# A message-passing layer's prologue: order of TensorE's and ScalarE's work, two weight loads and one group of gathers moved

## The chip, the cores and the metric

One NeuronCore of a Trainium2 chip runs the whole kernel. The metric is the device time of one execution in microseconds; a kernel's time is the median of several executions. Engines: TensorE (PE, with its weight loads as PEld), VectorE (DVE), ScalarE (ACT), GpSimd (POOL) and SyncE (SP), which here only issues DMAs. Transfers run on 16 DMA engines that all queues share.

## What is computed

1250 nodes with 512 features, 40000 edges sorted by destination, 64 features per edge. Cut to what matters:

```python
h = relu(layernorm(x))                                  # 1250 x 512
edge = concat([h[src], h[dst], edge_attr])              # 40000 x 1088
messages = mish(mish(edge @ W1 + b1) @ W2 + b2)         # 40000 x 512
agg = segment_sum(messages, dst)
u = mish(concat([h, agg]) @ W3 + b3)
x1 = x + layernorm(h + u @ W4 + b4) * gamma + beta
h2 = relu(layernorm(x1))
out = x1 + relu(segment_sum(((h2 @ U * s) @ Vt)[src] * w, dst) + bias)
```

## The kernel before

**Stages.** A prologue (time 0 to about 76 us) normalises x and makes two tables in DRAM: A = h @ W1[0:512], gathered later by `src`, and B = h @ W1[512:1024] + b1, read later by `dst`. The edge stage (about 76 to 1390 us) walks the edges in groups of 512 (four subtiles of 128): it gathers rows of A by an indirect DMA on GpSimd, transposes them on TensorE, adds B's rows and the edge part in the same PSUM bank (`bp`), applies mish, multiplies by W2 (`bm`, 12 products a subtile), applies mish again and sums by destination. Node and convolution stages end the kernel. Products are kept exact by splitting each operand in a high and a low part (`...h`, `...l`): a table row block is three times four products.

**Order.** Each engine has its own program, written out by hand, and executes in order; semaphores join them. x is cut in 10 chunks of 128 nodes, chunk numbers c = 0 to 9, that arrive in three batches, `BATCH` = chunks 0-1, 2-4 and 5-9.

**The prologue's program per chunk.** ScalarE makes relu(c) in place (`xs`/`hs`, L661). TensorE transposes it (L704, 4 instructions, bank `pT[c % 2]`). ScalarE copies the bank to `nTh` (`evac`, L470), VectorE subtracts for `nTl` (L614). TensorE makes the A product of the chunk (`table_a`, L681, 12 matmuls to `pA[c % 2]`: 4 with nTh and w1h, 4 with nTl, 4 with w1l). ScalarE copies `pA` to `ta` (`store_a`, L480) and SyncE issues its store to DRAM (L737). In TensorE's program the transposes of chunk c stand in front of the A product of chunk c-1. Ten B products (`pB`) follow the ten A products, and VectorE splits and stores them (L461 to L465, stores L761 and L762).

**VectorE between chunks.** After `nTl` of chunk c, VectorE runs the steps that the dictionary `between` lists for c: the statistics of the next batch (`variances`, `scales`), `windows` (waits for `dsti` and `dcoli`), `iotas`, the split of W1's second half (`w1_hi`, `w1_lo`), of W2 (`w2_hi`, `w2_lo`), `columns` (waits for `scoli` and `wcol`) and `bases`.

**SyncE's queue.** x batch 0, W1's first half (1 MB), x batches 1 and 2, x's tail of 98 rows, `dsti` (79 rows of 2 KB), `dcoli`, and then the A stores in order of chunk, with other loads behind some of them: W1's second half behind store 0, `wcraw` and W2 (1 MB) behind store 1, a wait for the windows and their store behind store 3, `scoli`, `wcol` and `b1b` behind store 4, `base_b` behind store 5. GpSimd issues zero fills of the result tables, one per transposed chunk (`agg_tab` for chunks 0 to 4, `M_tab` for 5 to 8).

**GpSimd in the edge stage.** In slot s it makes the low part of the hidden value of subtile s+4 (`low`, L985), then gathers for a group two ahead: for the third group (subtiles 8 to 11) rows 0 and 1 in slot -1, row 2 in slot 0, row 3 in slot 1, each behind the slot's `low`. The gathers of a group land on one semaphore, and TensorE starts on the group when all four have landed.

Of the kernel before, what the change touches and what calls it, by code (L numbers as in the profile page):

```python
# [23 lines left out]
ACT = mybir.ActivationFunctionType  # L24
# [4 lines left out]
KC = H // P  # L29
N = 1250  # L30
NCH = -(-N // P)
# [3 lines left out]
SUB = 4  # L35
# [181 lines left out]
def gnn_two_layers(nc, x, src_idx, dst_rows, src_cols, dst_cols, eaT, ew_cols, W1, b1, W2, b2, W3, b3, W4, b4,  # L217
# [39 lines left out]
    with ctx:  # L257
# [128 lines left out]
        with st:  # L386
# [52 lines left out]
            c_ta = sem("c_ta")  # L439
            c_tb = sem("c_tb")  # L440
            c_pad = sem("c_pad")
            v = {}
            prologue = Work()

# [22 lines left out]
            def evac(e, c):  # L467
                i = c % 2
                e.wait_ge(c_tr, c + 1)
                e.activation(nTh[:, :, c * P:(c + 1) * P], pT[i][:, :].rearrange("p (k n) -> p k n", k=KC),  # L470
                             ACT.Copy).then_inc(c_hi, 1)
                if c >= 1:
                    store_a(e, c - 1)

            def store_a(e, c):
                i = c % TA
                e.wait_ge(c_A, c + 1)
                if c >= TA:
                    e.wait_ge(q_sa[i], 16 * (c // TA))
                e.activation(ta[i][:], pA[c % 2][:, :], ACT.Copy).then_inc(c_ta, 1)  # L480

            @prologue.on("vector")
            def _(e):
                def link(ins):
                    c_v.inc(ins)
# [6 lines left out]
                def variances(i):  # L492

                    c0, c1 = BATCH[i]
                    e.wait_ge(q_x[i], (16, 16, 32)[i])
                    for c in range(c0, c1):
                        c_v.inc(e.bn_stats(stats[:, c, :], xs[:, c, :]))
                    later()
                    for c in range(c0, c1):
                        c_v.inc(e.bn_aggr(mv[:, c, :], stats[:, c, :]))  # L500
                    later()
                    link(e.tensor_scalar(var[:, c0:c1], mv[:, c0:c1, 1], LN_EPS, None, ALU.add))
                    v["var", i] = c_v.n
# [7 lines left out]
                                                ALU.mult, ALU.mult))  # L511
                    v["rstd", i] = c_v.n

                def w1_hi(i):

                    k = slice(i * KC, (i + 1) * KC)
                    e.wait_ge(q_w1[i], 16)
                    link(e.tensor_copy(w1h[:, k, :], w1raw[:, k, :]))
                    v["w1h", i] = c_v.n

                def w1_lo(i):

                    k = slice(i * KC, (i + 1) * KC)
                    c_v.inc(e.tensor_tensor(w1l[:, k, :], w1raw[:, k, :], w1h[:, k, :], ALU.subtract))
                    v["w1l", i] = c_v.n

# [25 lines left out]
                def w2_hi():  # L552

                    e.wait_ge(q_w2, 3 * 16)
                    c_v.inc(e.tensor_scalar(W2h[:], W2raw[:], -1.0, None, ALU.mult))
                    c_v.inc(e.tensor_copy(eaW2[:], wcraw[:]))
                    for i in range(2):
                        c_v.inc(e.tensor_copy(eaW1[i][64:128, :], wcraw[64:128, :]))

                def w2_lo():  # L560

                    later()
                    c_v.inc(e.scalar_tensor_tensor(W2l[:], W2raw[:], -1.0, W2h[:], ALU.mult, ALU.subtract))
                    c_v.inc(e.tensor_tensor(eaW2[64:128, :], wcraw[64:128, :], eaW2[64:128, :], ALU.subtract))

# [25 lines left out]
                def columns():  # L591
# [7 lines left out]
                    c_v.inc(e.scalar_tensor_tensor(scol8[:], rem[:], -float(EC), scolf[:], ALU.mult, ALU.add))  # L599
                    c_v.inc(e.tensor_tensor(wcol_hl[:, :, 1], wcol[:], wcol_hl[:, :, 0], ALU.subtract))  # L600

                between = {0: [lambda: variances(1), lambda: scales(1)], 1: [lambda: variances(2)], 2: [windows],
                           3: [lambda: scales(2), iotas], 4: [lambda: w1_hi(1)], 5: [lambda: w1_lo(1)], 6: [w2_hi],
                           7: [w2_lo], 8: [columns], 9: [bases]}

                e.memset(xs[:, NCH - 1, :], 0.0).then_inc(c_pad, 1)
                variances(0)
                scales(0)
                w1_hi(0)
                w1_lo(0)  # L610
                for c in range(NCH):
                    i = c % 2
# [34 lines left out]
            @prologue.on("scalar")  # L647
            def _(e):
                e.preload_act_table_set("natural_log_exp_and_others")
                for c in range(NCH):  # L650
                    for i in range(len(BATCH)):
                        c0, c1 = BATCH[i]
                        if c == (0, 2, 4)[i]:

                            e.wait_ge(c_v.sem, v["var", i])
                            e.activation(lnv[:, c0:c1], var[:, c0:c1], ACT.Ln).then_inc(c_a, 1)
                            e.wait_ge(c_a, 2 * i + 1)
                            e.activation(rstd[:, c0:c1], lnv[:, c0:c1], ACT.Exp, scale=-0.5).then_inc(c_a, 1)
                        if c == c0:
# [3 lines left out]
                    if c >= 1:  # L663
                        evac(e, c - 1)
                evac(e, NCH - 1)
                store_a(e, NCH - 1)

            @prologue.on("tensor")
            def _(e):
                e.wait_ge(c_g.sem, 4)  # L670

                def table(c, half, bank):

                    n = 0
                    for a, w, part in ((nTh, w1h, "w1h"), (nTl, w1h, None), (nTh, w1l, "w1l")):
                        if part and c == 0:
                            e.wait_ge(c_v.sem, v[part, half])
                        if half == 0 and a is nTl:
                            e.wait_ge(c_lo, c + 1)
                        for k in range(KC):  # L680
                            last = e.matmul(bank[:, :], a[:, k, c * P:(c + 1) * P], w[:, half * KC + k, :],  # L681
                                            start=n == 0, stop=n == 3 * KC - 1)
                            n += 1
                    return last

                def table_a(c):

                    e.wait_ge(c_hi, c + 1)
                    if c >= 2:
                        e.wait_ge(c_ta, c - 1)  # L690
                    table(c, 0, pA[c % 2]).then_inc(c_A, 1)

                def table_b(c):

                    if c >= TB:
                        e.wait_ge(c_tb, 3 * (c - TB) + 1)
                    table(c, 1, pB[c % TB]).then_inc(c_B, 1)

                for c in range(NCH):
                    e.wait_ge(c_hT, c + 1)  # L700
                    if c >= 2:
# [4 lines left out]
                    if c >= 1:  # L706
                        table_a(c - 1)
                table_a(NCH - 1)
                for c in range(NCH):
                    table_b(c)  # L710

            @prologue.on("sync")
            def _(e):
# [15 lines left out]
                        w1_half(0)  # L729
                e.wait_ge(c_pad, 1)  # L730
                e.dma_start(xs[0:NTAIL, NCH - 1, :], x[(NCH - 1) * P:N, :]).then_inc(q_x[-1], 16)
                e.dma_start(dsti[:], dst_rows).then_inc(q_dst, 16)
                e.dma_start(dcoli[:], dst_cols).then_inc(q_dst, 16)

                for c in range(NCH):
                    e.wait_ge(c_ta, c + 1)
                    e.dma_start(A_d[c * P:(c + 1) * P, :], ta[c % TA][:]).then_inc(q_sa[c % TA], 16)  # L737
                    if c == 0:
                        w1_half(1)
                    if c == 1:  # L740
                        for a, b in HALF:
                            e.dma_start(wcraw[a:b, :], W1[2 * H:2 * H + ED, :]).then_inc(q_w2, 16)
# [52 lines left out]
def edge_narrow(work, scope, sem, k):  # L795
# [36 lines left out]
    with st:  # L832
# [132 lines left out]
        def _(e):  # L965
# [45 lines left out]
                 .then_inc(q_adj, 16)  # L1011

            def step(s):
                if (s + DVE_PRE).has(PRES):
                    low(s + DVE_PRE)
                if s.j in GATHER_AHEAD:
                    ahead, ts = GATHER_AHEAD[s.j]
                    u = s + ahead
                    if u.reg is None and u.const == 4 * FULL:
                        ts = tuple(t for t in ts if t == 0)  # L1020
                    if s.reg is None and s.const in (-2, -1):
                        ts = (0, 1) if s.const == -1 else ()
                    if ts and u.has(MSGS) and not (u.reg is None and u.const < 2 * SUB):
# [1365 lines left out]
```

## Time and profile before

| | |
|---|---|
| median of 3 runs | 1532.44 us (1531.72 to 1532.98) |
| the profiled execution | 1531.4 us, its span 1529.7 us |
| busy share of the span | PE 98%, DVE 92%, ACT 85%, POOL 71% |
| chain that ended last | PE 84%, DVE 5%, issue 3%, DMA 3%, POOL 3%, ACT 1% |
| granted TensorE clock, mean | 0.996 of full speed |

A row of a timeline reads: start in us, duration, engine, line, operation, output<-input; in brackets the idle time of that engine just before, and what ended it. SPq is SyncE issuing a DMA, and its duration is that of the issue, not of the transfer. The profiled execution's own time is 1.0 us under the median of the runs.

### The profile page before, as it was taken

What the parts mean: (1) busy time and instruction counts of PE and PEld (TensorE: products, weight loads), DVE (VectorE), ACT (ScalarE), POOL (GpSimd) and SP (SyncE); (2) the same over time, 40 slices, a digit from 0 to 9 for tenths busy, and PEclk for the clock granted to TensorE, in tenths of its full rate; (3) what the DMA queues carried; (4) which work ended last, traced back from release to release, by engine and by line L of the source; (5) the groups of instructions that cost most, each with busy time, mean ns of one, the idle gap of its engine ahead of it and who ended that gap; (6) DMA issues with size and microseconds to landing.
All of it is one profiled execution on the core that took longest, in us unless ns stands there. A gap on an engine that the chain in (4) does not pass through costs nothing.

```text
span 1529.7 us, 33369 instructions
## 1 busy us (share of the span) xinstructions
PE 1494.8 (98%) x7862; PEld 1167.1 (76%) x7862; DVE 1414.1 (92%) x2924; ACT 1296.5 (85%) x2505; POOL 1082.4 (71%) x984
## 2 busy tenths in 40 slices
PE   7979999999999999999999999999999999999998
PEld 5767777777777777777777777777777777776785
DVE  7789999999999999999999999999999999995666
ACT  4079999999999999999999999999999999995462
POOL 2257888888878788787888878888887888763220
PEclk9999999999999999999999999999999999999999
DMA  8964555455455455545545445554554554545563
GB/s 314 313 195 115 118 124 124 114 128 117 116 125 123 117 118 124 123 114 127 117 115 129 119 117 121 122 124 117 124 119 117 128 116 116 125 124 132 133 151 148
DMA packets 122452, 205.10 MB, mean 134 GB/s; under 512 B 31641, under 2 KB 54297, under 8 KB 122416
## 3 DMA queue, kind: packets, MB, share of 16 engines
q0 software_dynamic: 59392, 116.85, 34.7%
q1 hardware_dynamic: 62672, 87.30, 18.3%
q10 hardware_dynamic: 352, 0.52, 0.1%
q8 instruction: 16, 0.26, 0.1%
q14 instruction: 20, 0.16, 0.0%
HBM read 151.60 MB, written 42.75 MB: 127 GB/s over the span
## 4 chain that ended last, share of the span: by engine, by line
PE 84%; DVE 5%; issue 3%; DMA 3%; POOL 3%; ACT 1%; POOLq 0%; DVEq 0%; SPq 0%; ACTq 0%
PE bm L1081 50%; PE bp L1060 7%; PE bp L1068 5%; PE bs L1104 4%; PE bp L1070 4%; PE pu L337 2%; PE pm L1092 2%; PE pu L2023 2%; PE po L2045 2%; DMA xg<-A_tab,idx 2%; PE pm L1091 1%; POOL hTl L985 1%; DMA Bl_tab<-tbl 1%; PE pA L681 1%; PE pu L2090 1%
## 5 line engine op out<-in xcount | busy, mean ns | idle before, releaser
L985 POOL TENSOR_TENSOR hTl<-tp,hTh 128x512 fp32r<-128x512 f32 (+1 forms) x314 | 411.2, 1309 | 215.5 <-DVE khl L1272 199.8
L1081 PE MATMUL bm<-W2h,hTh 128*128 128x512 f32 x1252 | 497.5, 397 | 1.9 <-POOL hTl L985 1.4
L1081 PE MATMUL bm<-W2l,hTh 128*128 128x512 f32 x1252 | 496.1, 396 | 0.0
L1081 PE MATMUL bm<-W2h,hTl 128*128 128x512 f32 x1252 | 494.1, 395 | 0.0
L974 POOL DMA_INDIRECT xg<-A_tab,idx x305 | 319.3, 1047 | 48.7 <-issue 41.0
L1081 PEld LDWEIGHTS bm<-W2h,hTh 128*128 128x128 f32 x1252 | 234.9, 188 | 71.0 <-DVE bm L1265 14.8
L1081 PEld LDWEIGHTS bm<-W2l,hTh 128*128 128x128 f32 x1252 | 235.2, 188 | 57.3
L1081 PEld LDWEIGHTS bm<-W2h,hTl 128*128 128x128 f32 x1252 | 235.1, 188 | 53.5
L1142 ACT ACTIVATE rp<-bp 128x512 f32<-128x512 f32 (+1 forms) x314 | 183.3, 584 | 105.3 <-PE bp L1070 74.4
L1236 DVE SCALAR_TENSOR_TENSOR rp<-rp 128x512 f32<-128x512 f32 (+1 forms) x314 | 215.3, 686 | 32.5 <-ACT rp L1142 19.3
L1246 DVE SCALAR_TENSOR_TENSOR tp<-rp,bp 128x512 f32<-128x512 f32 (+1 forms) x314 | 211.6, 674 | 4.7 <-ACT rp L1148 2.3
L1259 DVE SCALAR_TENSOR_TENSOR tm<-rm,bm 128x512 f32<-128x512 f32 x313 | 210.1, 672 | 3.4 <-ACT rm L1165 3.4
L1265 DVE COPY bm<-b2b 128x512 f32<-128x512 f32 x309 | 210.3, 680 | 0.0
L1145 ACT ACTIVATE rp<-rp 128x512 f32<-128x512 f32 (+1 forms) x314 | 195.5, 623 | 12.4 <-DVE rp L1236 6.4
L1161 ACT ACTIVATE rm<-rm 128x512 f32<-128x512 f32 x313 | 197.8, 632 | 5.0
L1163 ACT ACTIVATE rm<-rm 128x512 f32<-128x512 f32 x313 | 195.1, 623 | 0.1
L1165 ACT ACTIVATE rm<-rm 128x512 f32<-128x512 f32 x313 | 195.1, 623 | 0.1
L1148 ACT ACTIVATE rp<-rp 128x512 f32<-128x512 f32 (+1 forms) x314 | 194.0, 618 | 0.1
L1157 ACT ACTIVATE rm<-bm 128x512 f32<-128x512 f32 x313 | 185.0, 591 | 1.9 <-DVE tm L1259 1.8
L1060 PEld LDWEIGHTS bp<-ident_r,xg 128*128 128x128 f32 (+1 forms) x1244 | 123.8, 141 | 75.8 <-issue 40.3
L999 POOL DMA_DIRECT2D agg_tab<-ev x157 | 156.2, 995 | 25.3 <-DMA agg_tab<-ev 13.4
L1010 POOL DMA_DIRECT2D M_tab<-mev x157 | 164.7, 1049 | 9.2 <-issue 9.1
(246 smaller groups left out, 2312.8 us busy)
## 6 DMA issues: line engine op xcount, KB each, us to landing
ea<-in_eaT SPq DMA_DIRECT2D x156, 128.0 KB
M_tab<-mev POOLq DMA_DIRECT2D x157, 80.0 KB
agg_tab<-ev POOLq DMA_DIRECT2D x157, 64.0 KB
db<-in_dst_rows SPq DMA_DIRECT2D x78, 128.0 KB
M<-M SPq DMA_DIRECT2D x76, 128.0 KB
xg<-A_tab,idx POOLq DMA_INDIRECT x313
eaW<-Bh_tab SPq DMA_DIRECT2D x77, 64.0 KB
eaW<-Bl_tab SPq DMA_DIRECT2D x77, 64.0 KB
```

Source lines behind the costliest of these rows:

```text
L974: e.indirect_dma_start(out=xg[p][0:r, t, :].bitcast(F32), out_offset=None, in_=A_d, in_offset=bass.IndirectOffsetOnAxis(ap=idx[p][0:r, t:t ...
L985: e.tensor_tensor(hTl[p][:, j, 0:w], pick(u, start_t, tp)[:, 0:w], hTh[p][:, j, 0:w], ALU.subtract)\
L1060: e.matmul(bank[:, t * P:t * P + r].bitcast(F32R), xg[p][0:r, t, j * P:(j + 1) * P], ident_r[0:r, 0:r], start=t == 0, stop=False, is_trans ...
L1081: last = e.matmul(bank[0:r, :], a[p][:, c, j * P:j * P + r], w[:, c, :], start=False, stop=c == KC - 1 and w is W2l, skip_group_check=True)
L1145: e.activation(t, t, ACT.Ln, bias=1.0, scale=0.5 / (SQ * SQ)).then_inc(a_pre, 1)
L1161: e.activation(t, t, ACT.Square, bias=SQ, scale=SQ).then_inc(a_msg, 1)
L1163: e.activation(t, t, ACT.Ln, bias=0.5, scale=0.5 / (SQ * SQ)).then_inc(a_msg, 1)
L1165: e.activation(t, t, ACT.Exp, scale=-1.0).then_inc(a_msg, 1)
L1236: e.scalar_tensor_tensor(t, t, 2.0 * SQ, t, ALU.add, ALU.mult).then_inc(v_sq, 1)
L1246: e.scalar_tensor_tensor(t, pick(u, start_r, rp)[:, 0:w], 1.0, pick(u, start_bank, bp)[:, 0:w], ALU.subtract, ALU.mult).then_inc(v_pre, 1)
L1259: e.scalar_tensor_tensor(tm[m.const % MBUF][0:r, :], rm[m.const % 2][0:r, :], 1.0, bm[m.j][0:r, :], ALU.subtract, ALU.mult).then_inc(v_msg, 1)
L1265: e.tensor_copy(bm[m.j][:, :], b2b[:]).then_inc(v_bias, 1)
```

## The change

TensorE: where a batch of x begins (chunks 2 and 5, `FRESH`), the A product of the chunk before goes in front of the transposes. ScalarE: its program is written out; relu runs further ahead, the copy of chunk 1's transposes comes before the second batch's roots, and it takes over two conversions from VectorE, the high parts of W1's second half and of W2. VectorE: loses those two, computes the second and third batch's statistics in another order, and `columns` moves from behind chunk 8 to behind chunk 6, in front of W2's parts; `windows` moves behind `scales(2)` of chunk 3. SyncE: the load of W1's second half moves from behind A store 0 to behind x's tail, in front of `dsti` and `dcoli`. GpSimd in the edge stage: rows 0 and 1 of the third group's gathers go in slot -4, in front of the first `low`; row 2 in slot -1 and row 3 in slot 0, behind `low`.

```diff
-                between = {0: [lambda: variances(1), lambda: scales(1)], 1: [lambda: variances(2)], 2: [windows],
-                           3: [lambda: scales(2), iotas], 4: [lambda: w1_hi(1)], 5: [lambda: w1_lo(1)], 6: [w2_hi],
-                           7: [w2_lo], 8: [columns], 9: [bases]}
+                between = {0: [lambda: row_stats(1), lambda: variances(1)], 1: [lambda: scales(1), lambda: row_stats(2)],
+                           2: [lambda: variances(2)], 3: [lambda: scales(2), windows], 4: [iotas],
+                           5: [lambda: w1_lo(1)], 6: [columns], 7: [we_hi], 8: [w2_lo], 9: [bases]}
...
+                def w1_hi():
+
+                    e.wait_ge(q_w1[1], 16)
+                    e.activation(w1h[:, KC:2 * KC, :], w1raw[:, KC:2 * KC, :], ACT.Copy, scale=1.0).then_inc(c_w1h, 1)
+
+                def w2_hi():
+
+                    e.wait_ge(q_w2, 3 * 16)
+                    e.activation(W2h[:], W2raw[:], ACT.Copy, scale=-1.0).then_inc(c_w2h, 1)
+
+                roots(0)
+                relu(0)
+                relu(1)
+                evac(e, 0)
+                evac(e, 1)
+                roots(1)
+                relu(2)
+                store_a(e, 0)
+                relu(3)
+                evac(e, 2)
+                store_a(e, 1)
+                relu(4)
+                evac(e, 3)
+                roots(2)
+                store_a(e, 2)
+                evac(e, 4)
+                relu(5)
+                relu(6)
+                store_a(e, 3)
+                w1_hi()
+                for c in (7, 8, 9):
+                    relu(c)
+                    evac(e, c - 2)
+                    store_a(e, c - 3)
+                w2_hi()
+                evac(e, 8)
...
                 for c in range(NCH):
+                    if c in FRESH:
+                        table_a(c - 1)
                     e.wait_ge(c_hT, c + 1)
...
-                    if c >= 1:
+                    if c >= 1 and c not in FRESH:
                         table_a(c - 1)
...
                 e.dma_start(xs[0:NTAIL, NCH - 1, :], x[(NCH - 1) * P:N, :]).then_inc(q_x[-1], 16)
+                w1_half(1)
                 e.dma_start(dsti[:], dst_rows).then_inc(q_dst, 16)
                 e.dma_start(dcoli[:], dst_cols).then_inc(q_dst, 16)
...
-                    if c == 0:
-                        w1_half(1)
...
             def step(s):
+                if s.reg is None and s.const == -4:
+                    gather(At(None, 2 * SUB), (0, 1))
                 if (s + DVE_PRE).has(PRES):
                     low(s + DVE_PRE)
+                if s.reg is None and s.const in (-1, 0):
+                    gather(At(None, 2 * SUB), (s.const + 3,))
```

## Rows read from the trace of the kernel before

**Rows 1.** Windows: us, busy us (instructions) by engine, granted clock, DMA share, GB/s.
```profile
103.00:1380.00 1277.00, 1273.78 (x6760) 998.45 (x6759) 1240.09 (x2538) 1190.61 (x2310) 1019.71 (x913) 1.00 0.50 120
```
**Rows 2.** Waits up to 85 us: us in total, times, longest.
```profile
PE pA L681 <- DVE nTl L614: 2.0, 3, 1.0
```
**Rows 3.** The chain in order of time, 14 to 48 us: start, us, what.
```profile
24.33 0.44 PE pT L704 x4
24.77 2.79 PE pA L681 x12
...
35.97 6.87 DMA wcol<-in_ew_cols
...
42.86 0.33 DVE wcol_hl L594
...
46.07 2.12 PE pA L681 x8
```
**Rows 4.** Timeline of TensorE, ScalarE and VectorE, 15 to 25 us.
```profile
15.60 0.81 ACT L661 ACTIVATE xs<-xs,nmr,rstd 128x512 f32<-128x512 f32 x1 [1.10 <-DVE nmr L510]
...
16.47 0.66 PE L704 MATMUL pT<-ident,xs 128*128 128x128 f32 x4 [2.14 <-ACT xs L661]
...
22.07 0.67 DVE L531 TENSOR_REDUCE win<-dsti 79x2 f32<-79x512 int32 x1
...
24.69 0.68 DVE L614 TENSOR_TENSOR nTl<-pT,nTh 128x512 fp32r<-128x512 f32 x1
```
**Rows 5.** Timeline of SyncE's issues up to 43 us.
```profile
31.44 4.01 SPq L737 DMA_DIRECT2D A_tab<-ta  x1
35.49 0.43 SPq L748 DMA_DIRECT2D scoli<-in_src_cols  x1
```
**Rows 6.** DMA view, 15.6 to 17.6 us: 40 slices, then packets by queue (q1 SyncE's).
```profile
DMA  0101001010011000110010101001100101001010
...
q0 software_dynamic: 9, 0.03, 4.0%
q1 hardware_dynamic: 9, 0.02, 2.4%
```
**Rows 7.** DMA view, 20.95 to 21.4 us: packets by size.
```profile
DMA packets 64, 0.17 MB, mean 382 GB/s; under 512 B 2, under 2 KB 10, under 8 KB 64
```
**Rows 8.** Windows, a stretch with DMA full, columns as in rows 1.
```profile
8.00:10.00 2.00, 1.50 (x7) 1.53 (x8) 1.97 (x2) 1.44 (x3) 0.00 (x0) 1.00 1.04 397
```
**Rows 9.** Time from issue to landing, views of the tiles scoli and xs.
```profile
DMA to landing us min/median/max: 5.7/5.7/5.7
...
DMA to landing us min/median/max: 3.3/5.4/7.5
```
**Rows 10.** Groups by form up to 48 us: busy, mean ns; idle before.
```profile
L480 ACT ACTIVATE ta<-pA 128x512 f32<-128x512 f32 x9 | 5.4, 597 | 11.1 <-PE pA L681 11.1
...
L518 DVE CAST w1h<-w1l_raw 128x2048 fp32r<-128x2048 f32 x2 | 2.5, 1227 | 0.6 <-DMA w1l_raw<-in_W 0.6
...
L555 DVE TENSOR_SCALAR W2h<-W2l_raw 128x2048 fp32r<-128x2048 f32 x1 | 1.4, 1435 | 1.4 <-DMA W2l_raw<-in_W 1.4
```
**Rows 11.** Timeline of GpSimd and TensorE, 84 to 103 us.
```profile
84.03 1.65 POOL L985 TENSOR_TENSOR hTl<-tp,hTh 128x512 fp32r<-128x512 f32 x1 [15.29 <-DVE hTh L1252]
...
91.15 1.02 POOL L974 DMA_INDIRECT xg<-A_tab,idx  x1 [0.16 <-issue]
...
95.96 1.24 POOL L974 DMA_INDIRECT xg<-A_tab,idx  x1
...
98.83 0.97 POOL L974 DMA_INDIRECT xg<-A_tab,idx  x1 [0.15 <-issue]
...
102.46 0.51 PE L1060 MATMUL bp<-ident_r,xg 128*128 128x128 f32 x4 [2.40 <-DMA xg<-A_tab,idx]
```
**Rows 12.** Windows around TensorE's idle times, columns as in rows 1.
```profile
80.00:84.00 4.00, 0.46 (x5) 0.46 (x6) 3.39 (x7) 2.95 (x6) 0.00 (x0) 1.00 0.49 156
84.00:88.00 4.00, 3.67 (x13) 2.54 (x13) 3.93 (x6) 2.99 (x6) 3.24 (x3) 0.57 1.01 351
```

More of the change, by code:

```diff
@@ L441, in gnn_two_layers @@
             c_pad = sem("c_pad")
+            c_w1h = sem("c_w1h")
+            c_w2h = sem("c_w2h")
+            FRESH = [c0 for c0, _ in BATCH[1:]]
             v = {}
@@ L471, in evac @@
                              ACT.Copy).then_inc(c_hi, 1)
-                if c >= 1:
-                    store_a(e, c - 1)
             def store_a(e, c):
@@ L490, in later, with row_stats @@
                     e.wait_ge(c_v.sem, c_v.n)
-                def variances(i):
+                def row_stats(i):
                     c0, c1 = BATCH[i]
@@ L497, in variances @@
                         c_v.inc(e.bn_stats(stats[:, c, :], xs[:, c, :]))
+                def variances(i):
+                    c0, c1 = BATCH[i]
                     later()
@@ L512, in scales @@
                     v["rstd", i] = c_v.n
[L514 to L519, printed above, removed]
+                def w1_hi():
+                    e.wait_ge(q_w1[0], 16)
+                    link(e.tensor_copy(w1h[:, 0:KC, :], w1raw[:, 0:KC, :]))
+                    v["w1h"] = c_v.n
                 def w1_lo(i):
                     k = slice(i * KC, (i + 1) * KC)
+                    if i:
+                        e.wait_ge(c_w1h, 1)
                     c_v.inc(e.tensor_tensor(w1l[:, k, :], w1raw[:, k, :], w1h[:, k, :], ALU.subtract))
@@ L550, in iotas, with we_hi @@
                     c_v.inc(e.tensor_copy(iota_p[:], iop_i[:]))
-                def w2_hi():
+                def we_hi():
                     e.wait_ge(q_w2, 3 * 16)
-                    c_v.inc(e.tensor_scalar(W2h[:], W2raw[:], -1.0, None, ALU.mult))
                     c_v.inc(e.tensor_copy(eaW2[:], wcraw[:]))
@@ L562, in w2_lo @@
                     later()
+                    e.wait_ge(c_w2h, 1)
                     c_v.inc(e.scalar_tensor_tensor(W2l[:], W2raw[:], -1.0, W2h[:], ALU.mult, ALU.subtract))
@@ L600, in columns @@
                     c_v.inc(e.tensor_tensor(wcol_hl[:, :, 1], wcol[:], wcol_hl[:, :, 0], ALU.subtract))
-                between = {0: [lambda: variances(1), lambda: scales(1)], 1: [lambda: variances(2)], 2: [windows],
-                           3: [lambda: scales(2), iotas], 4: [lambda: w1_hi(1)], 5: [lambda: w1_lo(1)], 6: [w2_hi],
-                           7: [w2_lo], 8: [columns], 9: [bases]}
+                between = {0: [lambda: row_stats(1), lambda: variances(1)], 1: [lambda: scales(1), lambda: row_stats(2)],
+                           2: [lambda: variances(2)], 3: [lambda: scales(2), windows], 4: [iotas],
+                           5: [lambda: w1_lo(1)], 6: [columns], 7: [we_hi], 8: [w2_lo], 9: [bases]}
                 e.memset(xs[:, NCH - 1, :], 0.0).then_inc(c_pad, 1)
+                row_stats(0)
                 variances(0)
                 scales(0)
-                w1_hi(0)
+                w1_hi()
                 w1_lo(0)
@@ L649, in _, with roots, relu @@
                 e.preload_act_table_set("natural_log_exp_and_others")
-                for c in range(NCH):
-                    for i in range(len(BATCH)):
[L652 to L659, printed above, removed]
+                def roots(i):
+                    c0, c1 = BATCH[i]
+                    e.wait_ge(c_v.sem, v["var", i])
+                    e.activation(lnv[:, c0:c1], var[:, c0:c1], ACT.Ln).then_inc(c_a, 1)
+                    e.wait_ge(c_a, 2 * i + 1)
+                    e.activation(rstd[:, c0:c1], lnv[:, c0:c1], ACT.Exp, scale=-0.5).then_inc(c_a, 1)
+                def relu(c):
+                    for i in range(len(BATCH)):
+                        if c == BATCH[i][0]:
                             e.wait_ge(c_v.sem, v["rstd", i])
@@ L662, in _, with w1_hi @@
                                  scale=rstd[:, c:c + 1]).then_inc(c_hT, 1)
[L663 to L666, printed above, removed]
+                def w1_hi():
+                    e.wait_ge(q_w1[1], 16)
[22 more added lines that the diff above has]
+                store_a(e, 3)
+                w1_hi()
+                for c in (7, 8, 9):
[4 more added lines that the diff above has]
+                evac(e, 8)
+                store_a(e, 7)
+                evac(e, 9)
+                store_a(e, 8)
+                store_a(e, 9)
             @prologue.on("tensor")
@@ L674, in table @@
                     n = 0
-                    for a, w, part in ((nTh, w1h, "w1h"), (nTl, w1h, None), (nTh, w1l, "w1l")):
-                        if part and c == 0:
-                            e.wait_ge(c_v.sem, v[part, half])
+                    for a, w in ((nTh, w1h), (nTl, w1h), (nTh, w1l)):
+                        if c == 0 and a is nTh and w is w1h:
+                            e.wait_ge(*((c_w1h, 1) if half else (c_v.sem, v["w1h"])))
+                        if c == 0 and w is w1l:
+                            e.wait_ge(c_v.sem, v["w1l", half])
                         if half == 0 and a is nTl:
@@ L1020, in step @@
                         ts = tuple(t for t in ts if t == 0)
-                    if s.reg is None and s.const in (-2, -1):
-                        ts = (0, 1) if s.const == -1 else ()
-                    if ts and u.has(MSGS) and not (u.reg is None and u.const < 2 * SUB):
+                    if u.has(MSGS) and ts and not (u.reg is None and u.const < 3 * SUB):
                         gather(u, ts)
```

1 line of the change is left out of this document (removed).

## Prediction

> **What bounds the kernel.** Read first where TensorE is not busy. From 103 to 1380 us it is busy 1273.8 of 1277 us [rows 1], so this long stretch is bound by TensorE and hands on what it is given: a microsecond won or lost before 103 us is one at the end. The bound that decides "faster" or "slower" here is 0.2%, or 3.1 us, about what a measurement of this kernel can tell from no change. So the question is what TensorE's work up to 103 us becomes. Read next its waits there: 2.14 us for the relu of chunk 2 [rows 4] and 2.0 us, in three places, for low parts [rows 2]; then 2.40 us for the third group's gathers [rows 11]. Its rhythm between is 2.79 us for a product of 12 and 0.44 for the four transposes [rows 3]. Last, read which transfer comes late: the chain goes 6.87 us through `wcol` before `columns` and the last A product can go on [rows 3].
>
> **Part 1, the new order alone.** In front of chunk 2's transposes TensorE now makes A product 1. Its nTh copy and low part no longer wait for batch 1's roots, so it runs as soon as product 0 lets it, from about 14.2 (16.47 less the wait of 2.14 [rows 4], and products overlap by some 0.15) to 17.0 (2.79), and transposes 2 run at 17.0 instead of 16.5, but with a product already done: the 2.1 us are filled. Batch 1's relu starts 0.17 us later than its 15.60 [rows 4], because one low part of 0.69 goes in front of `scales(1)`, most of it in the time that ScalarE's roots took. ScalarE's order then leaves 0.45 us before transposes 3 and 0.3 before chunk 2's low part. If every load were there in time, chunk by chunk TensorE would start the B products at 44.4 instead of 48.0: **3.7 us earlier**, at most 4.1, the two waits together.
>
> **Part 2, conversions to ScalarE.** VectorE loses 1.23 and 1.44 us [rows 10]. No 128x2048 copy of ScalarE is in the trace; 128x512 takes 0.597, so four such are 2.4 us, and since the two-element roots take 0.2 the fixed part is paid once: 1.8 us is the other end. I take 1.8. The first stands at 25.4 to 27.2, beside TensorE's wait of part 3; without that cover it costs up to 1.0 before chunk 5's copy. The second stands before chunk 8's copy, beside the wait of part 4. Both cost nothing here, and bring nothing beyond part 1.
>
> **Part 3, W1's second half in front of `dsti`.** This is where I expect the change to pay. Between 15.6 and 17.6 us the DMA engines move 18 packets, and the slices show one at a time, nine of GpSimd's and nine of SyncE's in turn [rows 6]: a single DMA engine works, the others are done. What is left in SyncE's queue then is `dsti`. That the share of `dcoli` comes behind it shows at 20.95 to 21.4: eight packets between 512 B and 2 KB (10 less 2) [rows 7], of which `dcoli`'s are the only ones then due (1264 B rows). So both are in at 21.4, and VectorE starts `windows` at 22.07 with no wait [rows 4]: 0.7 us of room. Now 1 MB goes in front, on every engine: a full DMA moves 397 GB/s [rows 8], one engine 24.8, and 65.5 KB take 2.6 us. That gives 24.0. A zero fill of 512 KB is 1.3 us per engine and takes turns with it; those of chunks 2 and 3 are issued at 17.5 and 18.5 instead of 17.4 and 20.7, so up to two of them, 2.6 us, get in between where the stretch before ended ahead of them. `dcoli` is in between 24.0 and 26.7; I take 26.4, since both fills are out 5 us before.
>
> The Trainium skill (DMA: Bandwidth & Descriptors, section "Why a DMA increments its semaphore by 16 and not by 1") says that a copy is cut over the largest number of engines up to 16 that divides its row count; 79 is prime, so one. The trace agrees: one engine at work in [rows 6]. Were the rule not so here, `dsti` would be over in 0.4 us a share and rival A would be the forecast.
>
> VectorE reaches `windows` at 22.0 and stands until 26.4. Queued behind are the low parts of chunk 4 and all later steps. From the start of `windows` to the next low part 2.62 us pass (22.07 to 24.69), which lands 0.69 later [rows 4]: 26.4 + 3.3 gives 29.8, where TensorE asked for it at 25.7. **TensorE waits 4.1 us in A product 4**, and part 1 is gone: product 4 ends at 31.6 where it ended at 30.8 (24.77 + 2.79 + 0.43 + 2.79 [rows 3]).
>
> **Part 4, `columns` two chunks earlier.** It now needs `scoli` and `wcol` after chunk 6. They stand behind A store 4. From 31.6: transposes 5 (0.6), copy (0.65), then ScalarE's store copy ends at 33.4; the store is issued then, `scoli` at 33.8, `wcol` at 34.3. The issue of that store took 4.01 us before [rows 5], while W2 was still under way; now W2 is in at about 32.5, so I take 0.4. From issue to landing `scoli` took 5.7 and `wcol` 6.9 [rows 9, 3]; the shortest of any load, x's first, took 3.3 [rows 9]. So `wcol` lands at 40.0 (37.6 to 41.2). VectorE is there at 36.5 and waits. From landing to TensorE's restart 3.2 us pass (42.86 to 46.07 in [rows 3]), so A product 7 goes on at 43.2, where it asked at 40.3: **a second wait of 2.9 us**. Behind it come 1.86 (8 matmuls), 0.44, and two products of 2.79: the B products start at 51.1 instead of 48.0 (46.07 + 1.96), **3.1 us later**. In short the start is the landing of `wcol` plus 11.1. The B phase (27.9 us of matmuls, then the first subtiles) moves as a block: its A store and gathers shift by the same 3 us.
>
> **Part 5, the third group's gathers.** Before, row 3 is issued at 98.83, lands 3.5 us on, and TensorE, free at 100.07, waits 2.40 [rows 11]. Now rows 0 and 1 are issued ahead of the first `low`. Their indices are issued at 80.7 and are small; at 1.3 us a gather the first `low` starts at 84.6 instead of 84.03 [rows 11], and ends at 86.3, before TensorE asks for it at 86.7. Row 2 takes the old place at 91.15, row 3 the one at 95.96, and lands at 99.5. The wait goes. What is late next is VectorE, which is busy 1240 of 1277 us [rows 1] and follows only as fast as it can. I take **2.2 us**, between 0.5 and 2.4.
>
> **Sum.** +3.1 - 2.2 = +0.9 us. On the profiled execution of 1531.4 that is 1532.3; on the runs' median of 1532.44, which lies 1.0 above it, **1533.3**. As a formula: the landing of `wcol`, less 36.9, less part 5.
>
> **Rivals.** (A) Both loads are in time: `dsti`'s tail is not behind W1's second half, or comes quickly. Then -3.7 - 2.2 = -5.9, 1526.5. For it: batch 0 of x lands in 3.3 us, and DMAs idle from 15.5 to 18. Against it: [rows 6 and 7], which leave VectorE only 0.7 us of room. 15%. (B) The first wait is there, the second isn't, since the queue is emptier by 1 MB: `wcol` by 37.0. Then the B products start at 48.1, and -2.1 is left, 1530.3. 12%. (C) Slower: the one engine that carries `dsti` is busy without a break, since nothing is taken out of its queue, and `wcol` lands no sooner than the 42.86 of before. Each microsecond costs one; from 42.2 on the kernel is slower by over 3.1 us. Its price at 42.9 is +3.8, 1536.2. It gets help if the clock falls: after the idle stretch of TensorE from 80 to 83.5 us the granted clock is 0.57 for 84 to 88, against 1.00 before [rows 12], that is much of it at 1.2 GHz, and a wait of 4.1 us at 26 to 30 may bring the same, which puts the fourth store, and `wcol`, up to 1.7 us later: 40.0 becomes 41.7. Against it: fewer of the 640 KB fills come ahead. 18%. The forecast has 55%; its own range is 1531 to 1535.5.
>
> **Range and chances.** Beyond the forecast the range takes in B and C and most of A's edge: 1527.0 to 1536.5. Faster by over 0.2%: A and a little of B and the forecast's edge, 0.19. Slower by over 0.2%: C and the forecast's upper edge (`wcol` at 41.2 with 0.5 for part 5 gives +3.8), 0.21. Within: 0.60.
>
> **What the profile after would show.** Part 1: A product 1 before transposes 2, starting at 14.2. Part 3: VectorE idle before `windows`, ended by the DMA of `dsti` or `dcoli`, and TensorE idle about 4 us before the matmuls with nTl of chunk 4. Part 4: VectorE idle before `columns`, ended by `wcol`; the first pB matmul at 51. Part 5: no wait for xg near 100 us. A windows step that starts at 22 would make the prediction wrong by some 6 us in one stroke; a `wcol` that lands before 37 by 3.

## The result, and the profile after

The changed kernel takes 1539.73 us (median of 5 runs, 1538.91 to 1542.36) where the one before takes 1532.44: a ratio of 1.0052, 95% interval 1.0041 to 1.0063. It is **slower by 7.3 us**, forecast was 1533.3 with a range up to 1536.5. The profiled execution is the fastest of the five, 1538.91 us; its span of 1537.2 us is 7.5 above the span before. One execution of kernel 1 below (2013.08 us) and one of the kernel before timed beside it (7476.54 us) were in a slow state and enter no median or ratio here.

First, the long stretch. The same window of the kernel before, then of the kernel after, columns as in [rows 1]:

```profile
200.00:1380.00 1180.00, 1176.85 (x6251) 922.00 (x6249) 1146.86 (x2349) 1099.99 (x2136) 946.85 (x848) 1.00 0.51 120
...
200.00:1380.00 1180.00, 1176.97 (x6253) 923.31 (x6251) 1148.51 (x2349) 1102.04 (x2136) 950.57 (x851) 1.00 0.51 121
```

TensorE is busy 1176.85 us of it before and 1176.97 after. Nothing of the 7.5 us arises there; all of it is in front of it, as the reading of [rows 1] said. Next the chain of waits of the kernel after, in order of time, 5 to 60 us (start, us, what; steps of up to 0.04 us are left out without a mark); [rows 3] is its counterpart:

```profile
6.15 22.83 DMA dcoli<-in_dst_cols
...
29.07 0.68 DVE win L537
...
31.78 0.61 DVE nTl L621
...
32.43 3.78 PE pA L729 x8
36.21 0.73 PE pT L754 x4
36.99 0.42 issue
37.46 0.60 ACT ta L481
38.08 0.33 SPq L788
38.45 0.53 SPq L797
39.03 6.03 DMA wcol<-in_ew_cols
45.07 0.42 DVE wcol_hl L600
...
48.38 2.13 PE pA L729 x8
50.52 0.44 PE pT L754 x4
50.95 5.57 PE pA L729 x24
56.52 3.71 PE pB L729 x16
```

Both waits that the forecast put together its loss from are there, in its order. The chain leaves the load of `dcoli` at 29.0 us, runs through `windows` and chunk 4's low part to the eight matmuls, from these over A store 4 (line L788) to `wcol`, and over `columns` to A product 7. The timelines of VectorE and TensorE give the idle times (in brackets):

```profile
29.07 0.68 DVE L537 TENSOR_REDUCE win<-dsti 79x2 f32<-79x512 int32 x1 [7.37 <-DMA dcoli<-in_dst_cols]
...
45.07 0.42 DVE L600 CAST wcol_hl<-wcol 128x316 fp32r<-128x316 f32 x1 [3.99 <-DMA wcol<-in_ew_cols]
```

```profile
32.43 2.07 PE L729 MATMUL pA<-w1h,nTl 128*128 128x512 f32 x4 [6.70 <-DVE nTl L621]
34.30 1.91 PE L729 MATMUL pA<-w1l,nTh 128*128 128x512 f32 x4
...
48.38 1.21 PE L729 MATMUL pA<-w1h,nTl 128*128 128x512 f32 x4 [3.11 <-DVE nTl L621]
...
56.36 1.08 PE L729 MATMUL pB<-w1h,nTh 128*128 128x512 f32 x4
```

Four matmuls take 2.07 and 1.91 us behind the first wait, 1.21 behind the second. The windows tell why (us, busy us of PE, PEld, DVE, ACT, POOL, granted clock, DMA share, GB/s):

```profile
26.00:29.00 3.00, 0.00 (x0) 0.00 (x0) 0.00 (x0) 1.93 (x2) 0.00 (x0) 1.00 0.96 290
30.00:34.00 4.00, 1.57 (x4) 1.28 (x5) 2.89 (x16) 0.00 (x0) 0.00 (x0) 0.50 0.26 97
34.00:36.00 2.00, 2.00 (x6) 1.42 (x5) 0.00 (x0) 0.00 (x0) 0.00 (x0) 0.50 0.04 8
44.00:52.00 8.00, 4.89 (x26) 3.74 (x24) 6.73 (x13) 3.91 (x5) 0.71 (x1) 1.00 1.01 377
```

While TensorE stands (25.7 to 32.4 us), the granted clock falls to 0.50, 1.2 GHz, and is still there when the work comes back; it is 1.00 through the second wait. Last, the start of the B products and the edge stage. TensorE's timeline of the kernel before, where the third group's row is that of [rows 11]:

```profile
48.03 1.09 PE L681 MATMUL pB<-w1h,nTh 128*128 128x512 f32 x4
...
77.70 0.50 PE L1068 MATMUL bp<-M,eaW 128*128 128x512 f32 x1 [0.33 <-DMA eaW<-Bl_tab]
...
1384.05 0.45 PE L1081 MATMUL bm<-W2h,hTh 128*64 128x512 f32 x1 [0.51 <-DVE bm L1265]
```

and of the kernel after:

```profile
87.26 0.50 PE L1119 MATMUL bp<-M,eaW 128*128 128x512 f32 x1 [1.55 <-DMA eaW<-Bl_tab]
...
110.45 0.51 PE L1111 MATMUL bp<-ident_r,xg 128*128 128x128 f32 x4 [0.98 <-DMA xg<-A_tab,idx]
...
1391.72 0.45 PE L1132 MATMUL bm<-W2h,hTh 128*64 128x512 f32 x1 [0.51 <-DVE bm L1316]
```

The B products start at 56.36, 8.3 us later than before (48.03). The first product with B's rows stands at 87.26 instead of 77.70 (+9.6), since it waits 1.55 us for a B row where the kernel before waits 0.33. The third group starts 8.0 later (110.45 against 102.46), so 1.6 were given back in between; of that stretch the gathers' own wait shrank by 1.4, from 2.40 to 0.98. TensorE's last wait of the edge stage is at 1391.72 against 1384.05, +7.7.

### The profile page after: what moved, and what is told of

It reads as the page before. It is cut to its first block, busy times and chain, and to the rows that moved or that the text cites. A ratio compares the mean times of both kernels' runs of the same rounds, so it can differ in the third digit from the quotient of the medians.

```text
span 1537.2 us, 33369 instructions
## 1 busy us (share of the span) xinstructions
PE 1496.7 (97%) x7862; PEld 1168.2 (76%) x7862; DVE 1412.4 (92%) x2922; ACT 1300.2 (85%) x2507; POOL 1082.1 (70%) x984
## 4 chain that ended last, share of the span: by engine, by line
PE 79%; issue 5%; DVE 4%; DMA 4%; POOL 4%; ACT 1%; POOLq 1%; SPq 0%; ACTq 0%; DVEq 0%
PE bm L1132 48%; PE bp L1111 6%; PE bp L1119 5%; PE bs L1155 4%; PE bp L1121 4%; PE pm L1143 2%; PE pu L2074 2%; PE po L2096 2%; DMA dcoli<-in_dst_cols 1%; DMA xg<-A_tab,idx 1%; PE pu L337 1%; PE pm L1142 1%; POOL hTl L1034 1%; POOL M_tab L1059 1%; POOL agg_tab L1048 1%
```

## The experiments

Each kernel was timed beside the kernel before, in four sets on different chips: 2, 3, 4 and 11 (there the kernel before has a median of 1531.99), 1, 5, 6 and 9 (1532.44), 7, 8 and 10 (1533.02), and 12 (1531.86). So kernels of different sets are compared here by their distance to the kernel before, not by their medians. "B start" is TensorE's first matmul to pB in the profiled execution.

| kernel | B start | median | to before, us | ratio to before, 95% |
|---|---|---|---|---|
| before | 48.0 | 1532.44 | | |
| after | 56.4 | 1539.73 | +7.3 | 1.0052 (1.0041 to 1.0063) |
| 1 before, W1's half in front of `dsti` | 54.0 | 1539.10 | +6.7 | 1.0041 (1.0027 to 1.0054) |
| 2 before, new gathers | 47.9 | 1531.00 | -1.0 | 0.9994 (0.9985 to 1.0002) |
| 3 after, W1's half behind | 53.7 | 1538.56 | +6.6 | 1.0049 (1.0034 to 1.0064) |
| 4 after, `dsti` split | 53.8 | 1535.90 | +3.9 | 1.0028 (1.0018 to 1.0037) |
| 5 after, `columns` behind chunk 8 | 54.8 | 1538.12 | +5.7 | 1.0039 (1.0026 to 1.0053) |
| 6 after, both 4 and 5 | 46.8 | 1530.82 | -1.6 | 0.9993 (0.9985 to 1.0002) |
| 7 as 6, old gathers | 46.5 | 1532.73 | -0.3 | 1.0001 (0.9993 to 1.0010) |
| 8 as 6, W2's conversion sooner | 44.3 | 1530.80 | -2.2 | 0.9992 (0.9983 to 1.0001) |
| 9 before, `dsti` split | 46.3 | 1530.57 | -1.9 | 0.9988 (0.9979 to 0.9997) |
| 10 as 9, new gathers | 49.7 | 1531.77 | -1.3 | 0.9992 (0.9983 to 1.0001) |
| 11 after, work for TensorE in the wait | 57.4 | 1540.61 | +8.6 | 1.0054 (1.0041 to 1.0068) |
| 12 after, zero fills later | 57.6 | 1541.32 | +9.5 | 1.0056 (1.0038 to 1.0074) |

**1. The W1 move alone.** To the kernel before:

```diff
+                w1_half(1)
                 e.dma_start(dsti[:], dst_rows).then_inc(q_dst, 16)
...
-                    if c == 0:
-                        w1_half(1)
```

> The kernel before with one part of the change alone: W1's second half is issued behind x's tail in front of dsti and dcoli, not behind A store 0. Theory (this one move makes the first wait, whatever the order of the other engines): VectorE's windows step waits from 22 to 27 to 29 us, TensorE waits 4 to 6 us in A product 3, and the kernel is slower than before by 4 to 8 us, 1536 to 1540. Rival (the move costs only together with the new order of VectorE's steps): within 1 us of the kernel before.

Chain of waits:

```profile
5.91 21.73 DMA dcoli<-in_dst_cols
27.66 0.68 DVE win L531
...
31.02 3.78 PE pA L681 x8
```

One moved load makes nearly the whole loss: +6.7 us. TensorE waits 5.25 us, and the eight matmuls take 3.78 us, as in the kernel after; from 28 to 36 us the granted clock is 0.57. There is no second wait, since `columns` is still behind chunk 8.

**2. The gathers alone.** To the kernel before, the diff's `step` part.

> The kernel before with the third group's gathers reordered as in the change, and nothing else changed. Theory: TensorE's wait of 2.40 us near 102 us goes, in part taken back by VectorE's pace: 1.5 to 2.4 us less than 1532.4, about 1530.5. Rival (the wait moves to the next group, or the first low part is held up by two gathers in front of it): no difference, within 0.5 us of the kernel before.

```profile
101.15 0.51 PE L1062 MATMUL bp<-ident_r,xg 128*128 128x128 f32 x4 [0.78 <-DMA xg<-A_tab,idx]
```

This row of TensorE's timeline has a wait of 0.78 where [rows 11] had 2.40, and stands 1.3 us earlier. 1.0 us less in the median is not clear of noise: its interval reaches from 0.15% less to 0.02% more.

**3. W1's half behind the two loads again, in the changed kernel.**

```diff
-                w1_half(1)
                 e.dma_start(dsti[:], dst_rows).then_inc(q_dst, 16)
                 e.dma_start(dcoli[:], dst_cols).then_inc(q_dst, 16)
+                w1_half(1)
```

> The changed kernel with one part undone: W1's second half is issued behind dsti and dcoli instead of in front of them; everything else as changed. Theory (one DMA engine carries all of dsti, and what stands in front of it in SyncE's queue delays VectorE's windows step): the windows step starts at about 22 us with no wait instead of at 29.07, TensorE's wait of 6.7 us in A product 4 goes and with it the half clock behind it; the wait for wcol stays, since that engine has as much to carry as before: the B products start at 51 to 53 instead of 56.3, the kernel takes 1534 to 1537 us against 1539.7 of the changed one. Rival (the load's place makes no difference, DMAs are late because all 16 engines are full): windows still starts after 27 us, and the time stays within 1538.5 to 1541.

The wait for `dcoli` shrinks to 0.67 us, and the time does not come back (+6.6, and an interval that overlaps that of the changed kernel). ScalarE's timeline shows what is late next:

```profile
28.98 1.91 ACT L676 ACTIVATE w1h<-w1l_raw 128x2048 fp32r<-128x2048 f32 x1 [3.49 <-DMA w1l_raw<-in_W]
30.79 0.80 ACT L670 ACTIVATE xs<-xs,nmr,rstd 128x512 f32<-128x512 f32 x1
31.50 0.57 ACT L473 ACTIVATE nTh<-pT 128x512 fp32r<-128x512 f32 x1
```

With the load behind, ScalarE stands in its new conversion, and relu 7 and copy 5 stand behind it in its program. TensorE waits 3.2 us for that copy, and then 3.1 us for `wcol`, and the granted clock is 0.58 from 33 to 37 us and 0.66 from 43 to 48. So the W1 move had a purpose: the conversion on ScalarE needs the half by 25.3 us.

**4. The same loads in the new order, but `dsti` in two DMAs.**

```diff
-                e.dma_start(dsti[:], dst_rows).then_inc(q_dst, 16)
+                for a, b in ((0, 64), (64, NG)):
+                    e.dma_start(dsti[a:b, :], dst_rows[a:b, :]).then_inc(q_dst, 16)
...
-                    e.wait_ge(q_dst, 32)
+                    e.wait_ge(q_dst, 48)
```

> The changed kernel with dsti loaded by two DMAs, rows 0 to 63 and rows 64 to 78, instead of one of 79 rows; everything else as changed, the bytes and the place in the queue the same. Theory (79 rows go to one DMA engine; 64 and 15 rows go to 16 and 15): dsti and dcoli land before 20 us, windows starts at 22 with no wait, no single engine is left behind, so wcol lands some 4 to 5 us after its issue at about 30 and the B products start at 46 to 48 instead of 56.3: 1529 to 1532 us. Rival (bytes ahead of it in the queue are what delays dsti, however it is cut): windows starts at 27 or later, and the time is within 1 us of 1539.7.

VectorE reads `dsti` with no wait, with the same bytes in the same place of the queue. What held `dcoli` back was that all 79 rows sat on one engine. The Trainium skill's rule that the forecast cited (DMA: Bandwidth & Descriptors, "Why a DMA increments its semaphore by 16 and not by 1") gives 16 and 15 engines for 64 and 15 rows; the trace agrees in so far as the wait of 7.37 us is gone. But only 3.4 us come back (+3.9 instead of +7.3). The chain and TensorE's timeline:

```profile
30.14 9.69 DMA wcol<-in_ew_cols
...
43.06 3.78 PE pA L729 x8
46.84 0.85 PE pT L754 x4
47.69 6.24 PE pA L729 x24
```

```profile
43.06 2.07 PE L729 MATMUL pA<-w1h,nTl 128*128 128x512 f32 x4 [6.68 <-DVE nTl L621]
```

`wcol` is issued 8.9 us sooner than in the kernel after and lands 5.2 us sooner: the DMA share is 1.04 from 30 to 38 us, so it takes 9.69 us instead of 6.03. The long wait has moved from A product 4 to A product 7, and the low clock with it (0.57 from 38 to 44 us, 0.58 from 44 to 50).

**5 and 6. `columns` back behind chunk 8, without and with the split.**

```diff
-                           5: [lambda: w1_lo(1)], 6: [columns], 7: [we_hi], 8: [w2_lo], 9: [bases]}
+                           5: [lambda: w1_lo(1)], 6: [we_hi], 7: [w2_lo], 8: [columns], 9: [bases]}
```

In its former place `we_hi` and then `w2_lo` each run a chunk sooner.

> The changed kernel with VectorE's columns step back behind chunk 8, where the kernel before has it (W2's and the edge weights' parts move up to chunks 6 and 7); everything else as changed. Theory (two waits in series, the second because columns asks for wcol two chunks too soon): the wait of 6.7 us in A product 4 and the half clock behind it stay, the wait of 3.1 us in A product 7 goes and a short one of under 1 us is left in A product 9: the B products start at 53 to 54 instead of 56.4, 1536 to 1537.5 us. Rival (the second wait is not columns but the transfers as such, and moves to another step): the B products start within 1 us of 56.4 and the time stays at 1539 to 1540.5.

> The changed kernel with both undone: dsti in two DMAs of 64 and 15 rows, and columns back behind chunk 8. Theory (these two waits are all that the new order of the prologue loses; without them its own gain shows): no wait of over 1 us of TensorE between 9 and 75 us, granted clock 1.0 there, the B products start at 45 to 46 instead of 48.0 of the kernel before, 1528 to 1530 us. Rival (16 DMA engines are full up to 40 us, so a faster prologue only runs into the next transfer): another wait on a DMA appears before 50 us or before the first subtiles, and the time is within 1 us of 1532.

Alone, the undone part gives 1.6 us; with the split, 8.9 us, and the kernel is level with the one before. In the start of the B products: kernel 6 with neither wait has 46.8, the first alone (kernel 5) adds 8.0, the second alone (kernel 4) adds 7.0, and both together (the kernel after) add 9.6. The two waits cover for each other. Kernel 5 keeps the first with its clock fall, kernel 4 meets a second that has grown to 6.68 us; only with both gone is the time back. VectorE's and ScalarE's timelines of kernel 6 show the one wait left:

```profile
37.96 2.29 DVE L569 SCALAR_TENSOR_TENSOR W2l<-W2l_raw,W2h 128x2048 fp32r<-128x2048 f32 x1 [3.22 <-ACT W2h L681]
```

```profile
35.46 0.60 ACT L481 ACTIVATE ta<-pA 128x512 f32<-128x512 f32 x1 [1.44 <-PE pA L729]
35.95 1.91 ACT L681 ACTIVATE W2h<-W2l_raw 128x2048 fp32r<-128x2048 f32 x1
```

VectorE waits for ScalarE's conversion of W2, which stands in its program behind the store copy of chunk 6; that costs TensorE 1.74 us in A product 8. It does so in kernel 5 too (3.23 and 1.74 us there). This wait came with the edit of 5, which also moves `w2_lo` from behind chunk 8 to behind chunk 7: in the kernel after and in kernel 4, which have it behind chunk 8, VectorE doesn't wait for the conversion.

**7. Kernel 6 with the old order of the gathers.** The diff's `step` part undone.

> The changed kernel with dsti in two DMAs, columns behind chunk 8, and the gathers in their old order; the prologue as changed. Theory (the gathers are worth what they are in the kernel before): 1.0 to 1.5 us more than the same kernel with the new order of the gathers, 1531.5 to 1532.5, and TensorE waits 2 us or more for xg near 100 us. Rival (the gathers' wait is hidden elsewhere once the prologue is earlier): within 0.5 us of that kernel.

The wait for xg is 2.39 us instead of 0.80 in kernel 6, and the distance to the kernel before 1.3 us worse (-0.3 against -1.6): a second reading of part 5, though the two intervals overlap. Behind the wait the granted clock is 0.63 from 101 to 105 us.

**8. Kernel 6 with W2's conversion in front of store copy 6.**

```diff
                     evac(e, c - 2)
+                    if c == 9:
+                        w2_hi()
                     store_a(e, c - 3)
-                w2_hi()
```

> The changed kernel with dsti in two DMAs, columns behind chunk 8, and ScalarE's conversion of W2's high part moved in front of its A store copy 6 instead of behind store copy 6. Theory (in the version without this move VectorE waited 3.2 us for that conversion, TensorE 1.7 us behind it, and nothing else is left): the B products start at 44.8 to 45.5 instead of 46.8, 1 to 2 us less than the version without it, 1528.5 to 1530 us. Rival (TensorE's gain is taken back by the stores of A and B, as DMAs are full): the B products start earlier, but the first subtiles do not, and the time is that of the version without it, 1530.8.

The B products start at 44.31, which part 1 gave as 44.4 "if every load were there in time". TensorE's timeline then:

```profile
76.12 0.50 PE L1121 MATMUL bp<-M,eaW 128*128 128x512 f32 x1 [2.46 <-DMA eaW<-Bl_tab]
...
99.20 0.51 PE L1113 MATMUL bp<-ident_r,xg 128*128 128x128 f32 x4 [0.90 <-DMA xg<-A_tab,idx]
```

Of the 3.7 us only 1.6 are left at the first product with B's rows (77.70 before), which now waits 2.46 us for them. The third group is 3.3 us earlier, gathers included, and the ratio is that of kernel 6 within the intervals. In this profiled execution the edge stage's last wait is at 1381.31, 2.7 earlier than before, but what follows takes 147.6 us where the kernel before took 145.7. That tail was between 144.2 (kernel 10) and 148.0 us (kernel 2) in the profiled executions.

**9 and 10. The kernel before with `dsti` split, and the same with the new gathers.** The diffs of 4 and 2.

> The kernel before with dsti loaded by two DMAs of 64 and 15 rows. Theory (16 engines share the load evenly then, and wcol, for which VectorE waits 0.87 us and TensorE 0.98, lands up to 1 us sooner): 0 to 1 us less, 1531 to 1532. Rival (one engine's backlog of 6.6 us holds up every transfer behind it by so much): wcol lands 3 us sooner or more, both waits go, 1529.5 to 1531.

> The kernel before with dsti in two DMAs and the third group's gathers reordered; the rest of the prologue as before. Theory (the two are independent): the 1.9 us of the split and the 1.0 us of the gathers add up, 1529 to 1530 us. Rival (the earlier B products meet a clock that falls longer at the start of the edge stage, 6.8 instead of 3.4 us, and take the gathers' part back): 1530.5 to 1531.5.

The split alone gives 1.9 us. At 0.12% that is under the 0.2% bound; its ratio is the lowest of all and its interval, which ends at 0.9997, the only one wholly below 1, but it overlaps those of kernels 2, 6, 8 and 10. Up to 44 us the two programs are the same, and yet `wcol`, issued at 32.39 and 32.51, lands 7.1 and 11.1 us on, and the B products start at 46.3 and 49.7. So the landing of the same load behind full engines (DMA share 1.04 in both) differed by 4 us between these two executions. Kernel 10's wait of 2.04 us for it also took the clock to 0.50, from 48 to 51 us. These single profiles don't tell whether the two edits add up; and as its B products came later, not sooner, kernel 10 didn't test the rival either.

**11. 28 more matmuls in front of chunk 4's wait,** so that TensorE works through the first wait. Their results go nowhere.

```diff
                         if half == 0 and a is nTl:
+                            if c == 4:
+                                for i in range(28):
+                                    e.matmul(spare[:, :], nTh[:, i % KC, c * P:(c + 1) * P], w1h[:, i % KC, :],
+                                             start=True, stop=True, skip_group_check=True)
                             e.wait_ge(c_lo, c + 1)
```

> The changed kernel with 28 added products of nTh and w1h of chunk 4 into an unused PSUM bank, in TensorE's program between A product 4's first four matmuls and its wait for chunk 4's low part (about 6.5 us of work in the stretch of 25.7 to 32.4 in which TensorE stood idle); their result is not used. Theory (the granted clock fell to 0.50 behind this idle stretch, and the fall costs twice): the clock stays at 1.0, the 8 matmuls behind the wait take 1.9 instead of 3.8 us, A store 4 and wcol's issue come 2 us earlier, and the kernel takes 1.5 to 2.5 us less, 1537 to 1538.5. Rival (the clock's cost is covered by the later wait for wcol, since the one DMA engine sets its landing): the clock stays at 1.0 but wcol lands where it did, at 45, and the time stays within 0.7 us of 1539.7.

The chain, TensorE's timeline, and a window:

```profile
32.80 2.12 PE pA L733 x8
...
37.44 5.99 DMA wcol<-in_ew_cols
...
46.80 3.78 PE pA L733 x8
```

```profile
46.80 2.07 PE L733 MATMUL pA<-w1h,nTl 128*128 128x512 f32 x4 [3.12 <-DVE nTl L621]
```

```profile
46.00:52.00 6.00, 5.20 (x14) 4.22 (x15) 5.42 (x8) 1.13 (x2) 0.00 (x0) 0.50 0.78 286
```

The clock stays up in the first wait, the eight matmuls take 2.12 us, and `wcol` lands 1.6 us sooner, as the theory had it. Then TensorE waits 3.12 us in A product 7, as long as in the kernel after, but this time the clock falls: from there to the B products it takes 10.6 us instead of the 8.0 of the kernel after. The 1.6 us won were paid back with 2.6, and the B products start 1.1 us later.

**12. GpSimd's zero fills of chunks 2 to 4 wait for chunk 5's transposes.**

```diff
-                    e.wait_ge(c_tr, i + 1)
+                    e.wait_ge(c_tr, i + 1 if i < 2 else 6)
```

> The changed kernel, but GpSimd's zero fills of the scratch memory for chunks 2 to 4 wait until chunk 5 has been transposed, so that they no longer share an engine with the load of dsti. Nothing is left out of the computation. Theory (fills that reach the one engine first push dsti and so dcoli back): dcoli lands at about 25 us instead of 29.0, VectorE's wait for it shrinks from 7.4 to 3 to 4 us, TensorE's first long wait from 6.7 to about 3 us, and the B products start 2 to 4 us sooner than at 56.4; kernel 1535 to 1538 us. Rival (the fills don't matter, the engine is kept busy by the megabyte loads alone): windows are still read at about 29 us, kernel 1539 to 1540.5 us.

VectorE's timeline:

```profile
25.61 0.68 DVE L537 TENSOR_REDUCE win<-dsti 79x2 f32<-79x512 int32 x1 [4.01 <-DMA dcoli<-in_dst_cols]
...
43.62 0.33 DVE L600 CAST wcol_hl<-wcol 128x316 fp32r<-128x316 f32 x1 [6.36 <-DMA wcol<-in_ew_cols]
```

`dcoli` lands 3.5 us sooner, as the theory has it and its rival doesn't. The DMA view of this kernel at 27.5 to 28.9 us shows a single engine still at work, at one engine's rate; which one, the view doesn't say, but it fits the one that had `dsti` in its queue and is late with what stands behind:

```profile
DMA  0101010010101010010101001010101001010100
...
DMA packets 17, 0.03 MB, mean 25 GB/s; under 512 B 0, under 2 KB 0, under 8 KB 17
```

But the kernel's time did not follow: the fills, issued from 33.4 us on, now compete with `wcol`, which takes 8.25 us, and the expected gain of 2 to 4 us fell. TensorE waits 3.21 and 5.4 us, and both times the clock falls (to 0.50 from 30 to 32, 0.51 from 46 to 52).

## Why the prediction was wrong, point by point

**Part 1** was right. TensorE starts A product 1 at 14.34 (14.2), transposes 2 at 17.12 (17.0), and with all loads in time the B products start at 44.31 (44.4). That a gain there is one at the end is only partly so: the wait for B's rows takes back 2 us of it.

**Part 2** was right on the size, 1.90 us. "Cost nothing" held in the kernel after, where neither VectorE nor ScalarE waited for these conversions or their loads. It is bound to the order around them: W2's costs TensorE 1.74 us once `w2_lo` asks for it a chunk sooner (kernels 5 and 6), and that of W1's half binds the load's place in the queue (kernel 3). Whether they cost anything in the change's own order without the two waits, no run shows.

**Part 3, the step that failed first.** The mechanism was right, the size too small. `dcoli` was in at 29.0, not 26.4, beyond the upper bound of 26.7, and that is the whole of the 2.6 us by which TensorE's wait in A product 4 was missed (6.70 instead of 4.1). The count of zero fills was too low: two were counted, while those of chunks 2, 3 and 4, issued at 18.0 to 23.0 us, were all out before 29. Moving the three away brings 25.5, in the range of 24.0 to 26.7. Three of 32 KB per engine at the 24.8 GB/s of part 3 are 3.9 us, measured 3.5. What holds the last 1.5 us above 24.0 was not tried apart.

**The clock, the second step that failed.** Rival C named it and gave it 1.7 us, as help for a rival of 18%; the forecast's sum had it at zero. It belonged in the sum: the fall came in each kernel in which TensorE kept a long first wait (5.25, 6.28 and 6.70 us in kernels 1, 5 and after) and behind the shorter ones of kernels 3 and 12 (3.22 and 3.21). The eight matmuls took 3.78 us, where kernel 11 with the clock up has 2.12, and the transposes 0.73 instead of 0.44: 2.0 us. From TensorE's restart to the issue of `wcol` it took 6.60 us in the kernel after and 4.64 in kernel 11, which gives the same. (The forecast's 1.86 for the eight was itself 0.3 short.)

**The sum of both.** Store 4 was issued at 38.08 instead of 33.4, 4.7 late: 2.6 from `dcoli` and 2.0 from the clock make 4.6 of it. `wcol` took 6.0 us from its issue, between the 5.7 of [rows 9] and the 6.9 of [rows 3], and landed at 45.07 instead of 40.0. The formula "landing plus 11.1" gave 56.2; measured 56.36. So 4.7 of the 5.3 us by which the start of the B products was missed stand in front of A store 4, the rest in `wcol`'s landing (0.3) and small steps, and **part 4** failed in its input only. Kernel 4 shows what it would have met otherwise: issued at 30.1, `wcol` still lands at 39.8, behind full engines. Rival B (`wcol` by 37.0) had no room either.

**Part 5** had the right sign and was too large: 2.2 forecast; 1.6 in the kernel after (+9.6 to +8.0), 1.3 in kernel 2's profile and 1.0 in its median, 1.3 between 7 and 6.

**The rivals.** The result lies on C's side, beyond its price of 1536.2, but not by C's own mechanism: from 36 to 38 us no DMA engine was at work (share 0.00), so no engine was busy without a break. `wcol` came 2.2 us after the 42.86 of before because its issue was late, by part 3's `dcoli` first and by C's helper, the clock, second. The forecast's own sum with 5.3 us more gives 1533.3 + 5.3 + 0.6 (part 5) = 1539.2, against 1539.73. The range failed because it varied each landing by itself and held the clock's 1.7 us in one rival only; they are one chain, where each delay feeds the next. (The forecast's own upper end, given as 1535.5, comes to 1536.2 with the bounds that the text names, 41.2 and 0.5.)

## What to carry to other kernels

A small load can sit on a single DMA engine, as the 79 rows did here. A megabyte put in front of it then delayed it and the load behind it by several microseconds, since other queues' transfers joined in; before you reorder around such a load, try it split, here into 64 and 15 rows. Price a TensorE wait with the half clock that may stand behind it (2.0 to 2.6 us here), and follow the delayed work through each later issue up to the wait that ends last. Two waits on one path cover for each other, so undo them together before you judge either.

## What the runs showed of the hardware

- Whether the clock falls in a wait is not a matter of that wait's length alone in these runs. In A product 7, a wait of 3.11 us left it at 1.00 in the kernel after (where it had been at 0.50 until 36 us), and one of 3.12 us took it to 0.50 in kernel 11 (where it had been at 1.00 before). It also fell behind waits of 3.21 us (kernel 12), 3.10 (kernel 3, A product 7) and 2.04 us (kernel 10). What decides was not settled.
- Keeping TensorE at work through a wait kept the clock up there (2.12 us for eight matmuls against 3.78), and brought the kernel nothing.
- The time from issue to landing of the same 158 KB load, `wcol`, with the DMA share in the 3 to 5 us before its issue: share about 0.2, 6.0 (after, kernel 11), 6.1 (kernel 5) and 8.25 us (kernel 12, with the moved fills beside it); share about 0.7, 4.9 (kernel 1) and 5.8 us (kernel 3); share 0.9 or more, 6.2, 6.7, 6.9, 7.1, 9.5, 9.7, 10.1 and 11.1 us (kernels 8, 2, before, 9, 7, 4, 6, 10). In kernel 4 an issue 8.9 us sooner was worth 5.2 us.
- ScalarE's copy of 128x2048 takes 1.90 us, less than four of 128x512 (2.4 us by [rows 10]).
